# Two transformer layers on one core: zeros of the relative rows, loads of pairs 2 and 3, and SP's order in layer 1's experts moved

## Time and profile before

| what | us |
|---|---|
| median of 3 runs | 1145.63 |
| the runs | 1145.63, 1151.29, 1142.08 |
| the profiled execution | 1143.02 |
| its span in the trace | 1141.1 |

### The profile page before, as it was taken

How to read it: one execution, slowest core, us unless ns; L and a number is a source line. 1 busy time by engine, 2 the same in 40 slices (tenths; PEclk the granted TensorE clock), 3 DMA queues, 4 the chain that set the end, 5 groups by cost and what they waited for, 6 DMA issues and landing times. The chain is left out here.

```text
span 1141.1 us, 22305 instructions
## 1 busy us (share of the span) xinstructions
PE 1032.1 (90%) x7828; PEld 643.7 (56%) x7828; DVE 756.0 (66%) x1707; ACT 728.8 (64%) x1087; POOL 541.1 (47%) x707
## 2 busy tenths in 40 slices
PE   3699999999998758999999999999999889999997
PEld 2444444677785434555555555554444466878785
DVE  7135342478865566787788888877786257676766
ACT  1479988556555326777777777777775655545453
POOL 1257776575543231333355544444222277555564
PEclk9979999999999857999999999999999999999999
DMA  4621141544664497888888888887672576433333
GB/s 160 225 79 51 57 128 32 151 124 141 164 192 154 157 264 228 241 244 241 242 254 261 250 248 238 242 240 243 217 225 62 146 195 131 120 117 122 116 123 91
DMA packets 146430, 197.41 MB, mean 173 GB/s; under 512 B 33292, under 2 KB 113149, under 8 KB 146285
## 3 DMA queue, kind: packets, MB, share of 16 engines
q1 hardware_dynamic: 126254, 184.32, 52.7%
q0 software_dynamic: 20064, 11.66, 5.8%
HBM read 123.00 MB, written 72.74 MB: 172 GB/s over the span
## 5 line engine op out<-in xcount | busy, mean ns | idle before, releaser
L1089 DVE TENSOR_REDUCE a_part<-a_duo 128x2 f32<-128x1024 f32 (+3 forms) x256 | 215.3, 855 | 13.5 <-PE a_duo L962 11.9
L755 POOL DMA_DIRECT2D scr_y1c<-ys x240 | 118.9, 504 | 207.7 <-DVE ys L1070 204.8
L1082 DVE CUSTOM_DVE_ANT_0 a_band_sum<-a_duo,a_rel_raw 128x256 f32<-128x256 f32 (+2 forms) x320 | 131.4, 448 | 79.6 <-PE a_duo L962 59.2
L1526 POOL TENSOR_TENSOR f_hid_lo<-f_hid,att 128x512 fp32r<-128x512 f32 (+1 forms) x100 | 129.7, 1298 | 104.7 <-ACT att L1495 104.7
L706 ACT ACTIVATE a_probs<-a_duo 128x1024 f32<-128x1024 f32 x192 | 140.2, 828 | 25.5 <-PE a_duo L655 24.3
L975 PE MATMUL a_duo<-att 32*128 32x512 f32 (+3 forms) x672 | 138.1, 408 | 17.0 <-DVE a_part L1089 12.8
L962 PE MATMUL a_duo<-att 31*128 31x512 f32 (+3 forms) x672 | 144.8, 427 | 9.4 <-PEq L1131 4.3
L1042 ACT ACTIVATE a_rel<-a_rel_ps 128x384 f32<-128x384 f32 x240 | 117.5, 490 | 47.5 <-PE a_rel_ps L949 45.3
L1658 DVE TENSOR_TENSOR f_hid<-f_u,w_share 128x512 f32<-128x512 f32 (+1 forms) x168 | 116.3, 692 | 32.0 <-DMA w_share<-scr_cw 9.4
L644 POOL TENSOR_TENSOR a_probs<-a_probs,const 128x256 f32<-128x256 f32 x128 | 101.7, 811 | 60.9 <-ACT a_probs L706 60.8
L1526 POOL TENSOR_TENSOR f_hid_lo<-f_hid,f_hid_hi 128x512 fp32r<-128x512 f32 x68 | 87.9, 1292 | 79.7 <-ACT f_hid_hi L1495 79.6
(11 more groups left out here) (268 smaller groups left out, 2049.3 us busy)
## 6 DMA issues: line engine op xcount, KB each, us to landing
a_rel_raw<-scr_rel SPq DMA_DIRECT2D x128, 384.0 KB, 4.4
scr_rel<-a_rel SPq DMA_DIRECT2D x120, 384.0 KB, 3.6
w_share<-scr_cw SPq DMA_DIRECT2D x144, 128.0 KB, 3.1
w_share<-scr_cw SPq DMA_DIRECT2D x44, 256.0 KB, 3.2
scr_y1c<-ys POOLq DMA_DIRECT2D x240, 8.0 KB, 3.7
w_share<-scr_cw SPq DMA_DIRECT2D x20, 192.0 KB, 2.9
w_share<-scr_cw SPq DMA_DIRECT2D x16, 224.0 KB, 3.0
att<-scr_q SPq DMA_DIRECT2D x36, 96.0 KB
```

Source lines behind the costliest of these rows:

```text
L755: eng.dma_start(scr["y1c"][w, b, head, :, at:at + T // 4], sb["ys"][32 * (2 * hd + c) + HD * w:32 * (2 * hd + c) + HD * (w + 1), h % 2, :] ...
L1082: ins = dve.tensor_tensor_reduce(band_sum[:, m % 2, hd, 0:wide], both[:, hd, (a - 4 * x) * P:(b - 4 * x) * P], rel_raw[:, e % RING, hd, (a ...
L1089: ins = dve.tensor_reduce(part[:, h % 2, x, :, j % 4], both[:, :, lo * P:hi * P], AX.X, ALU.max, negate=True)
L1526: pool.tensor_tensor(hid_lo[0:m, n % 4, :], hid[0:m, n % 2, :], f32(hid_hi[0:m, n % 4, :]), ALU.subtract).then_inc(lo_ready, 1)
```

## The change

The zeros' DMA moves from the end of `prepare` to pair 2 of the sigmoid attention's loop on SP, behind the loads of pair 6 and ahead of the y stores of pair 2's second half. In the softmax attention POOL copies v first, waits until eight S scores are made, and then issues the loads of pairs 2 and 3. In the experts, `LOAD` is 3K + 4 in place of 3K + 6 (this acts in layer 0). In layer 1 the raw weight groups 2 to 5 are issued at n = 7, 10, 13 and 16 in place of 4, 7, 10 and 13; at each n the share goes ahead of the weights; and the wait for the stored y with the y loads moves from before the loop to n = 9.

```diff
@@ prepare, SP
             store(1)
-            sp.wait_ge(zeroed, 1)
-            sp.dma_start(scr["rel"][:, :, :, 0:P - 1].rearrange("s h p u -> p (s h) u"),
-                         view(zeros, [0, 32], [1, P - 1])).then_inc(ahead.guarded, 16)
@@ sigmoid_attention, SP
                     for hd in range(2):
                         load(pair + 4, hd)
+                if pair == 2:
+                    sp.wait_ge(ahead.zeroed, 1)
+                    sp.dma_start(scr["rel"][:, :, :, 0:P - 1].rearrange("s h p u -> p (s h) u"),
+                                 view(sb["cwT"][:, 0:P], [0, 32], [1, P - 1])).then_inc(ahead.guarded, 16)
@@ softmax_attention, POOL
+            copy_v(0)
+            copy_v(1)
+            pool.wait_ge(s_ready, 8)
             for pair in range(2, 4):
                 for hd in range(2):
                     for name, dst in (("q1h", qs), ("kah", ka), ("kbh", kb)):
                         load(pair, hd, name, dst)
-            copy_v(0)
-            copy_v(1)
@@ experts
-        load_at = {(1 + GRP * (g - 1) if EARLY else starts[g - 2]): g for g in range(2, len(groups))}
+        load_at = {(1 + GRP * g if EARLY else starts[g - 2]): g for g in range(2, len(groups))}
@@
-        FILL, LOAD, REL, LOGITS = 6, 3 * K + 6, 3 * K + 7, 3 * K + 4
+        FILL, LOAD, REL, LOGITS = 6, 3 * K + 4, 3 * K + 7, 3 * K + 4
@@ experts, SP
-            for s, n in enumerate(y_counts):
-                sp.wait_ge(y_stored[s], n)
             if k == 0:
+                for s, n in enumerate(y_counts):
+                    sp.wait_ge(y_stored[s], n)
@@
-            else:
-                for w, t_ in enumerate((yv, ysum)):
-                    sp.dma_start(flat(t_).rearrange("p (b t) -> p b t", b=B), scr["y1r"][w]).then_inc(att_loaded, 16)
             for n in range(M + TAIL):
-                if n in load_at:
-                    load(load_at[n])
                 if WB <= n < M:
                     sp.wait_ge(hid_ready, n - WB + 1)
                     share_out(weights, scr, sp, share, n)
+                if n in load_at:
+                    load(load_at[n])
+                if k == 1 and n == 9:
+                    for s, count in enumerate(y_counts):
+                        sp.wait_ge(y_stored[s], count)
+                    for w, t_ in enumerate((yv, ysum)):
+                        sp.dma_start(flat(t_).rearrange("p (b t) -> p b t", b=B), scr["y1r"][w]).then_inc(att_loaded, 16)
```

More of the change, by code:

```diff
@@ L196, in sem @@
             return ctx.enter_context(nc.semaphore("ahead_" + name))
-        self.guarded, self.qk_stored = sem("guarded"), sem("qk_stored")
+        self.zeroed, self.guarded, self.qk_stored = sem("zeroed"), sem("guarded"), sem("qk_stored")
         self.qk_loaded = [sem(f"qk_loaded{s}") for s in range(4)]
@@ L343, in prepare @@
         gw_ready, logits_ready, exp_in, exp_ready = sem("gw_ready"), sem("logits_ready"), sem("exp_in"), sem("exp_ready")
-        step, zeroed = sem("step"), sem("zeroed")
+        step = sem("step")
         ident = sb["const"][:, C_ID:C_ID + P]
         x, xn, x_hi, x_lo = sb["x"], sb["xn"], sb["x_hi"], sb["x_lo"]
-        zeros = sb["cwT"][:, 0:P]
         flat = xn[:].rearrange("p t d -> p (t d)")
@@ L423, in _ @@
             pool.memset(cw[:, :, E:E + 1], 1.0).then_inc(router.ones_set, 1)
-            pool.memset(zeros, 0.0).then_inc(zeroed, 1)
+            pool.memset(sb["cwT"][:, 0:P], 0.0).then_inc(ahead.zeroed, 1)
             pool.wait_ge(const_loaded, 16)
```

## The result

| | before | after |
|---|---|---|
| median of 4 runs each, us | 1146.58 (1142.08 to 1151.29) | 1133.80 (1131.28 to 1136.52) |
| the profiled execution | 1143.02 | 1134.96 |
| its span | 1141.1 | 1133.0 |

The ratio is 0.9889, with a 95% interval of 0.9841 to 0.9936: 12.7 us faster, where 19.4 were forecast. The time lies in the range given, 7.8 above the forecast. The span fell by 8.1 us. Split at the stages' first matmuls, before against after: layer 0's experts begin at 208.31 against 196.44 (-11.9); that stage takes 198.93 against 195.41 (-3.5); the softmax attention 491.95 against 497.74 (+5.8); layer 1's experts 241.91 against 243.41 (+1.5). Two stretches got shorter, as forecast, and two got longer.

The account below looks back on a forecast made before the run. TensorE, busy nine tenths at full clock, bounds the kernel; only its pauses and the slow clock behind them can be won. 11.5 + 4.0 + 2.0 + 1.9 = 19.4 us off 1143.0 gives 1123.6, as median 1126; range 1117 to 1137.

Parts of the forecast that it names:

- Part 1: Sigmoid attention: zeros leave the front of SP's queue, removing 4.5 us of pause and 7.0 of slow clock; gain 11.5.
- Rival (a): Sigmoid attention: the zeros only move their stall, 2 us of pause and 7 of clock; gain 10.4, 1135 us; chance 0.07.
- the 15.8 us allowed: Sigmoid attention: time from the zeros' issue until TensorE needs the vector copy that waits for a y store behind them.
- Part 2: Layer 0's tail: first loads for layer 1 two chunks earlier, shortening TensorE's 3.40 us pause and its half clock; gain 4.0.
- The wait of 1.0 that was to remain: Layer 0's tail: 2.4 off TensorE's 3.40 us pause leaves 1.0, which should not drop the clock.
- its 1.6 for the half clock: Layer 0's tail: eight or nine matmuls at half clock behind the 3.40 us pause cost about 1.6 us more.
- Part 3: Softmax attention's start: POOL's twelve loads behind the eighth S bring the row of maxima earlier; gain 2.0, bounds -4.7 and 4.7.
- By turns, about half of POOL's bytes are still ahead of the row: Softmax start: with DMA engines alternating between queues, POOL's loads still partly delay the row of maxima; gain 2.0 of at most 4.7.
- Part 4: Layer 1's experts: each share ahead of the weights removes DVE's share waits; gain 1.9, bounds -2 and 4.
- The ring: Layer 1's experts: a work cycle through POOL, TensorE and ACT sets 7.93 us per three chunks, 39.65 for five threes.
- that one may be a microsecond late. I leave the term at 1.9: Layer 1's experts: the second weight load, behind y's 2 MB, may be a microsecond late; the gain stays 1.9.
- rival (d): Layer 1's experts: weight loads come late each time, costing 24.8 against 17.5 gained; 7 us slower, 1153; chance 0.03.

Follow-up runs that it names:

- POOL at 15: The changed kernel with POOL waiting for the row of maxima's store before its loads of pairs 2 and 3; median 1130.95 us, 0.9850 of the kernel before.

## Why the prediction was right, and where it was wrong

**Part 1, -11.5: right.** Four pairs gave 11.4, the stage's end 11.9. The margin of 3 us held: TensorE didn't wait for pair 1's loads. The rule of the Trainium skill cited there (DMA: Bandwidth & Descriptors, "Why a DMA increments its semaphore by 16 and not by 1"), by which a load of 3 x 8 rows goes over three engines, held again: 0.19 at 78 GB/s in the window shown. Rival (a) fell, but not with the 6 us to spare that were worked out. The copy that TensorE needs came 13.6 us after the zeros' issue in after and 14.4 in the profile of the changed kernel run again, and at 14.4 TensorE already waited 0.28 for it: the 15.8 us allowed were too many, and the ten taken as likely too few. That this cost nothing is in part luck. What was mis-sized is how well one execution stands for the others: layer 0's experts begin at 206.6 in the mean of the four profiles with the zeros in front (208.3, 203.3, 210.8, 203.9) and at 196.7 in the mean of the ten with them moved (195.9 to 197.4). The part is worth 9.9 in the mean.

**Part 2, -4.0: right in size.** 3.5 in the profiled pair; means of 198.8 (four profiles with the old `LOAD`) and 195.7 (seven with the new one and the logits unmoved): 3.1. The wait of 1.0 that was to remain was 0.92 to 1.43 where the clock was full, without a half clock behind it, as forecast. In after itself the clock fell ahead of the wait and hid it. What the prediction did not see is that its 1.6 for the half clock and its remaining wait are not separate terms.

**Part 3, -2.0: wrong in sign.** The step that failed is "By turns, about half of POOL's bytes are still ahead of the row". Its first half, that the reads and the first store come faster, was right (4.3 us at the row's issue). But nearly all of POOL's bytes were still ahead of the row, not half: eleven of the twelve loads had landed by 417.5, and the row was used at 419.01. From POOL's first issue on, SP's queue held the three relative stores and a read ahead of the row, up to 1.5 MB, against POOL's 1.15 MB; two queues that move the same amount in the same time let all of the smaller amount through. In the order before, all twelve loads had landed too (the last at 429.5) before the row was used at 432.39, so the change took none of their bytes from ahead of it. Putting them behind the row (POOL at 15) did, and gave 4.2 to 5.5 us at the first T (22.45 against 26.67 to 27.97), about the 4.7 us that the prediction had as the most this part could win. The Trainium skill (DMA: Bandwidth & Descriptors, "Queues, rings and completion order") says that an engine takes turns packet by packet between the queues with work. The 1.14 and 1.06 MB of the two queues from 404 to 416 us are what turns could give; the rows don't name a packet's engine, so the turns themselves aren't shown. The half doesn't follow from them.

In time this part was +1.5 with an interval through zero: the first T came 1.9 later in the mean, yet the first copy of the accumulator, some 20 us behind, came at 45.4, 45.5, 50.8 and 51.0 with the old order and at 48.0 to 49.0 with the changed one, means of 48.2 and 48.4. The two late ones of the old order (50.8 and 51.0) are the two in which the granted clock stayed at half until 52 and 53 us into the stage; in the two early ones it rose at 36. Why it rose later in the first two wasn't tried. With POOL at 15 the copy comes at 44.4 to 46.2 in all six profiles.

**Part 4, -1.9: not won.** The ring was right: 39.71 to 39.76 for chunks 4 to 19 in all six kernels whose weights come in time, against the 39.65 worked out. The step that failed is "that one may be a microsecond late. I leave the term at 1.9". It was 3.6 late, and the last group 2.2 late. In the means of four, the old order took 41.95 and the changed one 42.96: +1.0, with ranges that overlap (41.0 to 43.1 and 41.9 to 43.7), so the missing gain is clear and the loss isn't. It is rival (d)'s mechanism, at one place (chunk 10) in each of the four profiles and at a second (chunk 16) in two, instead of at each load. The clock held in after; in the kernel with POOL at 15 the weights for chunk 10 were 4.2 late, TensorE paused 1.60 us for ACT behind it, and the clock was at half for some 7 us. The value taken for the landing was at fault: the earlier trace rows gives 3.7 us in the middle, and behind y the weights took up to 8.3 in after (8.9 with POOL at 15). The rows held a hint: the 5.6 us at the top of the earlier trace rows belong to the load at 911.52, which stood next behind y in before.

**Sum.** -9.9, -3.1, +0.3 to +1.9 and +1.0 make -10 to -12, and the two measurements of the change are -12.7 and -10.5. The 5.8 us that the softmax attention lost in the profiled pair are 2.9 up to the first copy (more than the mean's 0.3), and one stall of 2.9 in the middle of the stage, behind this wait of after's TensorE:

```profile
643.32 0.49 PE L976 MATMUL a_duo<-att 32*128 32x512 f32 x2 [1.30 <-DMA att<-a_rows]
```

The same code has such stalls at other places or not at all, and the stage took 492.0 to 500.2 us in the four profiles whose softmax is as before. Nothing is to be read from one such number.

## What to carry to other kernels

Before a transfer is moved, count the bytes that are ahead of the one you want early, in its own queue and in the other, from the moment the other starts. Here a 2 KB row behind up to 1.5 MB of its own queue let nearly all of the other's 1.15 MB ahead of it, so bulk loads without haste go behind it, not just later than before. When an order is turned round to free one stream (shares), ask the same of the stream that now stands behind (weights), with landings taken under the load they will meet, and put what is needed last (y) last. And a stall followed by a slow clock is worth a range and not a number: its pause is alike in each execution, what follows it isn't.

## What was unexpected of the hardware

- The granted clock fell to its half level (1.2 of 2.4 GHz) behind 24 matmuls of 16 columns with no gap between them, with TensorE counted as busy 2.00 of 2.00 us ahead of it (0.54 in the window 330 to 332 of after), in five of twelve profiles.
- Behind one and the same stall of TensorE (4.5 to 6.1 us) the half clock cost 3.4, 3.4, 8.5 and 12.0 us in four profiles.
- The same transfer lands later beside others: the 2 KB row took at most 5.7 us from issue to use at a DMA share of 0.42 (409 to 414 us) and 10.6 at one of 1.11. The slowest weight load took 8.3 us behind y's two loads in after, 5.6 before.
- A DMA of 4096 pieces of 508 bytes held up the next issue in its queue at both of its places, 8.83 us before and 8.95 in after, where its neighbours take 0.7 or less.
